# DLRM tower: in the last two batches, four channels of an outer product move to GpSimd, two sums move to VectorE, and the tail steps change places

## The reference, cut to what matters

```python
for i in range(3):                                    # xk = e at first
    z = einsum('bfe,bge->bfge', x, xk)                # outer products over the 16 fields
    z = relu(einsum(z, Ws[i]) + bs[i]).sum(-1)        # 16 numbers per sample
    xk = broadcast(z)                                 # so layers 1 and 2 need only y = x @ Ws[i].T and z
h = concat([z0, z1, z2, dense_ctx], axis=1)           # 48 + 16 = 64 features
h = relu(h @ W_top1 + b_top1)                         # 512
h = relu(h @ W_top2 + b_top2)                         # 256
y = h @ W_top3                                        # 1
```

## Time and profile before

| | |
|---|---|
| median of 3 runs | 578.62 us (578.22 to 579.26) |
| the profiled execution | 579.74 us |
| its span in the profile | 578.0 us |
| VectorE busy | 542.8 us (94%) |
| ScalarE busy | 498.7 us (86%) |
| TensorE matmuls busy | 476.3 us (82%) |
| GpSimd busy | 467.8 us (81%) |
| TensorE's mean granted clock | 0.956 of 2.4 GHz |

### The profile page before, as it was taken

How to read it: one execution, slowest core, us unless ns; L and a number is a source line. 1 busy time by engine, 2 the same in 40 slices (tenths; PEclk the granted TensorE clock), 3 DMA queues, 4 the chain that set the end, 5 groups by cost and what they waited for, 6 DMA issues and landing times.

```text
span 578.0 us, 10773 instructions
## 1 busy us (share of the span) xinstructions
PE 476.3 (82%) x3990; PEld 190.8 (33%) x3990; DVE 542.8 (94%) x326; ACT 498.7 (86%) x1471; POOL 467.8 (81%) x354
## 2 busy tenths in 40 slices
PE   5559888687888798878989788798869888789988
PEld 5213233232333333232333323233333323233324
DVE  1697999999999999999999999999999999999994
ACT  1143698999999999999999999989999999999875
POOL 6665888889888888888888889888888888888630
PEclk9689898999989989998999999799999989999979
DMA  3352212221222122212221222212212212210000
GB/s 98 92 145 74 75 56 57 63 64 56 74 58 64 56 71 72 67 56 74 62 64 56 69 60 61 73 57 82 64 56 66 61 60 74 57 54 1 1 2 0
DMA packets 14334, 35.43 MB, mean 61 GB/s; under 512 B 5493, under 2 KB 5879, under 8 KB 14266
## 3 DMA queue, kind: packets, MB, share of 16 engines
q0 software_dynamic: 12288, 33.57, 20.3%
q1 hardware_dynamic: 1994, 1.17, 0.8%
HBM read 34.71 MB, written 0.01 MB: 60 GB/s over the span
## 4 chain that ended last, share of the span: by engine, by line
DVE 38%; ACT 28%; PE 18%; issue 10%; POOL 3%; another core or an unknown queue 1%; DMA 1%; ACTq 0%; DVEq 0%; POOLq 0%
DVE prod L436 32%; ACT outer L637 15%; PE z_ps L827 8%; DVE outer L485 6%; ACT outer L627 3%; ACT sq L582 3%; POOL x_rows L342 3%; PE t_ps L790 3%; ACT relu L593 2%; ACT xt L574 2%; PE turn_ps L898 1%; PE turn_ps L902 1%; PE turn_ps L860 1%; PE zs_ps L842 1%
## 5 line engine op out<-in xcount | busy, mean ns | idle before, releaser
L436 DVE TENSOR_TENSOR prod<-t_ps,xt 128x2048 f32<-128x2048 f32 x190 | 420.8, 2281 | 11.0 <-remote 6.7
L342 POOL DMA_INDIRECT x_rows<-in_tbl,ids_sb x256 | 248.4, 970 | 73.1 <-issue 62.0
L637 ACT ACTIVATE outer<-outer,bias_sb 128x256 f32<-128x256 f32 x476 | 236.7, 518 | 3.0 <-DVE outer L485 3.0
L827 PE MATMUL z_ps<-prod,w_sb 128*32 128x512 f32 x1520 | 191.2, 622 | 37.3 <-DVE prod L436 34.3
L356 POOL TENSOR_TENSOR intra<-xt 128x1024 f32<-128x1024 f32 (+4 forms) x90 | 205.1, 2281 | 6.0 <-PE z_ps L827 4.5
L574 ACT ACTIVATE xt<-t_ps 128x512 f32<-128x512 f32 x128 | 75.2, 604 | 45.2 <-PE t_ps L790 21.7
L637 ACT ACTIVATION_READ_ACCUMULATOR outer<-outer,bias_sb 128x1 f32 x476 | 100.2, 210 | 0.0
L485 DVE TENSOR_TENSOR outer<-y_ps,z_all 128x1408 f32<-128x1408 f32 (+2 forms) x60 | 93.4, 1598 | 4.5 <-ACT outer L627 3.5
L790 PE MATMUL t_ps<-ident,x_rows 128*128 128x128 f32 x512 | 81.2, 288 | 19.0 <-DMA x_rows<-in_tbl,ids_sb 7.1
L827 PEld LDWEIGHTS z_ps<-prod,w_sb 128*32 128x32 f32 x1520 | 45.8, 111 | 124.8 <-issue 93.3
L790 PEld LDWEIGHTS t_ps<-ident,x_rows 128*128 128x128 f32 x512 | 55.9, 143 | 81.8 <-issue 59.6
(11 more groups left out here) (69 smaller groups left out, 219.1 us busy)
## 6 DMA issues: line engine op xcount, KB each, us to landing
x_rows<-in_tbl,ids_sb POOLq DMA_INDIRECT x256
w_sb<-in_w SPq DMA_DIRECT2D x1, 512.0 KB
feat<-in_dense SPq DMA_DIRECT2D x1, 128.0 KB
w_sb<-in_w SPq DMA_DIRECT2D x1, 128.0 KB
ids_sb<-in_ids SPq DMA_DIRECT2D x1, 120.0 KB
ident<-in_identity SPq DMA_DIRECT2D x1, 64.0 KB, 2.1
w_sb<-in_w0t SPq DMA_DIRECT2D x1, 64.0 KB
sel_sb<-in_sel SPq DMA_DIRECT2D x1, 48.0 KB
```

Of the source, the lines that this page charges most:

```text
L342: pool.indirect_dma_start(out=x_rows[:, par, f, :], out_offset=None, in_=tables[f], in_offset=bass.IndirectOffsetOnAxis(ap=ids_sb[:, NF * ...
L436: dve.tensor_tensor(prod[:, m % PROD_RING, half, :].rearrange("p (f g s) -> p f g s", f=QF, g=QF), t_ps[:, tbank(b, q, half), :, :].unsque ...
L637: act.activation(outer_of(b)[:, o // OP, o % OP, :], outer_of(b)[:, o // OP, o % OP, :], ACT.Relu, bias=bias12_sb[:, layer - 1, o:o + 1], ...
L827: mm = pe.matmul(z_ps[j * GR:(j + 1) * GR, m % 2, 0:n], w0_sb[:, half, slot, :], src[:, half, j * n:(j + 1) * n], start=(slot == 0 and hal ...
```

## The change

- GpSimd gets `outer_former`: channels 12 to 15 of batch 14's layer 2 outer product. It reads a copy of y in SBUF that ScalarE makes with a new `copy_y_former`, between `copy_tile(LAST, 3, 1)` and `move_z0(LAST - 1)`. VectorE's second piece of that outer product shrinks from 8 channels to 4. VectorE's four sums (14, 2) wait for GpSimd.
- VectorE takes 12 of the 16 sums (15, 1) instead of 10, ScalarE 4 instead of 6.
- On ScalarE, the move of `mlp_b` goes ahead of `sum_outer(14, 2, 8, 12)`; the eight sums (15, 2) all go ahead of the move of `mlp_c`, and of `tail_move(0, 4)` and `(0, 5)`, which stood between them.
- On TensorE, `mlp_c` goes from ahead of `tail_h2(0, .)` to behind it; `form_feat(LAST)` goes ahead of `tail_y(0)`; the eight transposes at the end are gone.

```diff
-WARM = {"first": 28, "second": 22, "end": 8}
+WARM = {"first": 28, "second": 22}
-VECTOR_SUMS = {(2, 2): 4, (1, 1): 10, (1, 2): 8}
+VECTOR_SUMS = {(2, 2): 4, (1, 1): 12, (1, 2): 8}
+        y_former = sb("y_former", [P, QF, GROUPS, LAST_OP])
-        def vector_channels(b):
+        def vector_channels(b, layer):
-            return NF - LAST_OP if b == LAST else NF
+            return NF - LAST_OP if (b, layer) > (LAST - 1, 1) else NF
@@ gpsimd
+            def outer_former():
+                pool.wait_ge(y_copied, 1)
+                pool.wait_ge(z_ready, z_count(LAST - 1, 1))
+                o = NF - LAST_OP
+                y = y_former[:, :, :, :].rearrange("p f c o -> p o (f c)")
+                pool.tensor_tensor(
+                    outer[:, o // OP, o % OP:o % OP + LAST_OP, :].rearrange("p o (g f) -> p o g f", g=NF),
+                    y.unsqueeze(2).to_broadcast([P, LAST_OP, NF, NF]),
+                    z_all[:, (LAST - 1) % 2, 1, :].unsqueeze(1).unsqueeze(3).to_broadcast([P, LAST_OP, NF, NF]),
+                    ALU.mult).then_inc(pool_outer, 1)
             multiply_last_unit(1)
+            outer_former()
             outer_last(1)
@@ vector
-                n = op(b)
+                n = min(op(b), vector_channels(b, layer) - o)
                     else:
-                        dve.wait_ge(pool_outer, layer)
+                        dve.wait_ge(pool_outer, 1 if b < LAST else 1 + layer)
-            vector_sum(LAST, 1, 6, 16)
+            vector_sum(LAST, 1, 4, 16)
@@ scalar
+            def copy_y_former():
+                act.wait_ge(y_turned, LAST)
+                act.activation(y_former[:, :, :, :], y_ps[:, :, :, 1, NF - LAST_OP:NF], ACT.Copy).then_inc(y_copied, 1)
             copy_tile(LAST, 3, 1)
+            copy_y_former()
             move_z0(LAST - 1)
...
             sum_outer(LAST - 1, 2, 4, 8)
+            mlp_in(LAST, "mlp_b")
             sum_outer(LAST - 1, 2, 8, 12)
-            mlp_in(LAST, "mlp_b")
             move_feat(LAST - 1)
             sum_outer(LAST, 1, 0, 2)
             sum_outer(LAST, 1, 2, 4)
-            sum_outer(LAST, 1, 4, 6)
             tail_move(0, 0)
             tail_move(0, 1)
             tail_move(0, 2)
             tail_move(0, 3)
+            sum_outer(LAST, 2, 0, 4)
+            sum_outer(LAST, 2, 4, 8)
             mlp_in(LAST, "mlp_c")
-            sum_outer(LAST, 2, 0, 2)
-            sum_outer(LAST, 2, 2, 4)
             tail_move(0, 4)
             tail_move(0, 5)
-            sum_outer(LAST, 2, 4, 6)
-            sum_outer(LAST, 2, 6, 8)
             move_feat(LAST)
@@ tensor
             tail_h1(0, 3)
-            mlp_in(LAST, "mlp_c")
             tail_h2(0, 0)
             tail_h2(0, 1)
             tail_h2(0, 2)
             tail_h2(0, 3)
+            mlp_in(LAST, "mlp_c")
+            form_feat(LAST)
             tail_y(0)
-            pe.wait_ge(turn_moved, turn(LAST + 2, "feat"))
-            keep_warm("end")
-            form_feat(LAST)
             tail_h1(1, 0)
```

More of the change, by code:

```diff
@@ L212, in op @@
             return LAST_OP if b == LAST else OP
-        def vector_channels(b):
-            return NF - LAST_OP if b == LAST else NF
+        def vector_channels(b, layer):
+            return NF - LAST_OP if (b, layer) > (LAST - 1, 1) else NF
         def piece(b, layer, o):
-            return 2 * PIECES * b + vector_channels(b) // op(b) * (layer - 1) + o // op(b)
+            return 2 * PIECES * b + vector_channels(b, 1) // op(b) * (layer - 1) + o // op(b)
         def mlp_slot(frame, kind):
@@ L368, in multiply_last_unit @@
                     ALU.mult).then_inc(pool_multiplied, 1)
+            def outer_former():
[8 more added lines that the diff above has]
+                    ALU.mult).then_inc(pool_outer, 1)
             def outer_last(layer):
                 if layer == 1:
-                    pool.wait_ge(y_copied, 1)
+                    pool.wait_ge(y_copied, 2)
                     pool.wait_ge(z0_moved, NB)
@@ L478, in outer_piece @@
                         dve.wait_ge(y_turned, b + 1)
-                        if b == LAST:
-                            dve.wait_ge(y_copied, 1)
+                        if b >= LAST - 1:
+                            dve.wait_ge(y_copied, b - LAST + 2)
                     if (b, layer) != (LAST, 1):
@@ L491, in outer_pieces @@
             def outer_pieces(b, layer):
-                for o in range(0, vector_channels(b), op(b)):
+                for o in range(0, vector_channels(b, layer), op(b)):
                     outer_piece(b, layer, o)
@@ L498, in vector_sum @@
                 for o in range(first, last):
-                    if o < vector_channels(b):
+                    if o < vector_channels(b, layer):
                         dve.wait_ge(outer_done, piece(b, layer, o) + 1)
                     else:
-                        dve.wait_ge(pool_outer, layer)
+                        dve.wait_ge(pool_outer, 1 if b < LAST else 1 + layer)
                     dve.scalar_tensor_tensor(
@@ L949, in keep_warm @@
             def keep_warm(when):
-                out = turn_ps[:, 0:P] if when == "end" else zs_ps[:, 0:P]
                 for _ in range(WARM[when]):
-                    pe.transpose(out, ident[:, :], ident[:, :])
+                    pe.transpose(zs_ps[:, 0:P], ident[:, :], ident[:, :])
             pe.wait_ge(ident_loaded, 16)
```

## The result

| | before | changed |
|---|---|---|
| median | 579.26 us (574.37 to 582.61, 19 executions) | 582.93 us (580.17 to 586.45 and one of 674.55, 19 executions) |
| ratio of the two | | 1.0078, 95% interval 1.0053 to 1.0104 |
| profiled execution | 579.74 us | 581.73 us |
| its span | 578.0 us | 579.6 us |

One of the 19 executions of the changed kernel took 674.55 us, with a mean clock of 0.735 against 0.91 to 0.96 in the others; it is left out of the ratio, and so are three of the experiments' (586.0 and 586.57 us with the gap filled, 586.75 us for GpSimd and VectorE alone), each over 1.5% above the fastest of its kernel.

The account below looks back on a forecast made before the run. The end was taken as set by `tail_h1(0, 0)`'s start, TensorE's 9.84 us and clock, and the step to `tail_h1(1, 0)`: 557.03 + 9.84 + 4.3, then 2.4, 5.8 and 1.74, gave 581.1, forecast 581.0 us; range 578.9 to 582.8.

Parts of the forecast that it names:

- The part on GpSimd and VectorE: Batch 14 outer product split and sums (15, 1): z of layer 1 ready 2.0 us earlier, hidden behind `mlp_c`.
- ScalarE's wait for `mlp_b`: ScalarE stands 1.4 us for `mlp_b`'s matmuls; `tail_h1(0, 0)` starts at 557.03 instead of 555.58, 1.45 us later.
- The step from `mlp_c`'s end to `tail_h1(1, 0)`: In the tail, `tail_h1(1, 0)` starts 2.4 us after `mlp_c` ends, behind its move and two queued tail moves.
- The whole tail without low clock: With equal clock loss in both kernels, the tail step `tail_h1(1, 0)` starts 0.5 us later than before.
- The low clock over all of `tail_h1`: TensorE's clock at 0.50 from about 557 to about 566, covering `tail_h1` from its start.
- Rivals 3 to 5: TensorE clock stays up, 576.8 us (0.10); last 128 samples at low clock, 583.3 (0.06); GpSimd holds VectorE up, 583.5 (0.04).
- the term L: Time lost to low clock from `tail_h1(0, 0)` to `mlp_c`'s end: 4.3 us taken, bounds 1.7 and 5.1.
- the sum: `mlp_c` ends at 571.2, `tail_h1(1, 0)` starts at 573.6, span ends at 579.4; with 1.74 us outside, 581.1.

Follow-up runs that it names:

- with the gap filled: Changed kernel plus 16 transposes that nobody reads, on TensorE between `mlp_b`'s matmuls and `form_feat(14)`; ratio to the kernel before 1.0026.
- GpSimd and VectorE alone: Kernel before plus `outer_former`, `copy_y_former` and VectorE's 12 sums (15, 1), all ScalarE and TensorE orders as before; ratio 1.0037.
- with `mlp_b` back and the gap filled: Changed kernel with `mlp_b`'s move behind its four sums again and 8 transposes between `mlp_b`'s matmuls and `form_feat(14)`; ratio to before 0.9998.
- e5_before_b_fwd: Kernel before with ScalarE's `mlp_b` move put ahead of the sums (14, 2) of channels 8 to 11; ratio 1.0075.
- the fastest version: Changed kernel, `mlp_b` behind its sums, 8 transposes ahead of `form_feat(14)` and 3 behind, `mlp_c` inside `tail_h1(0)`; 576.64 against 579.67 us, ratio 0.9957.

## Why the prediction was wrong

Right, by its own steps:

- The part on GpSimd and VectorE, and that its 2 us would be hidden: `form_feat(LAST)` came 5.5 us after the last sum.
- ScalarE's wait for `mlp_b`: 1.4 us expected, 1.39 measured. `tail_h1(0, 0)`: expected 12.14 us behind the tail's entry (557.03 - 544.89), measured 12.21.
- The step from `mlp_c`'s end to `tail_h1(1, 0)`: 2.4 expected, 573.82 - 571.3 = 2.5 measured. The whole tail without low clock: 0.5 us longer expected, 0.6 measured.
- The low clock over all of `tail_h1`, from about 557 to about 566: measured 556.1 to 566.4, 10.2 us. The span was expected at 579.4 and measured at 579.6, and that closeness is luck: the execution entered its tail 0.7 us earlier than before's had, and this hid a low stretch that cost 0.8 us more than the sum had.
- Rivals 3 to 5 did not happen: no profile of the changed kernel kept its clock up, the last 128 samples ran at 1.00, and VectorE's pieces of (14, 2) were not held up (3.42 us beside `outer_former`, 3.4 expected).

Wrong was the term L, the time lost to the low clock, in two ways. First its size: "I take 4.3" with 5.1 as the upper bound, and the three profiles of the changed kernel gave 5.1, 5.1 and 3.4, so the value taken as the extreme came twice in three. That is 0.8 us for the profiled execution. (About 0.2 of the 5.1 is not the clock's: the stretch from `tail_h1`'s start to the end of `mlp_c`, 9.84 us at full clock by the sum, took 10.0 us, 566.32 - 556.31, in the profile with `mlp_b` back and the gap filled, which has the same order and no low clock.) Secondly, and more, the step from the profile to the median: "in the changed kernel I expect the long stretch to be the rule, so I shift it hardly". The sum was made against one execution of before that itself had lost 3.4 us to the low clock, while its second profile lost nothing. So it gave the changed kernel 4.3 - 3.4 = 0.9 us of clock, and by leaving out the 1.1 us between that execution and before's median nearly 1 us more: before was taken to lose 2.3 to 2.4 us as a rule. The moved line lengthens the low stretch and also makes it regular: the profiles with `mlp_b` forward and nothing in the gap lost 5.1, 5.1, 3.4 and 4.7 us (in the last, `e5_before_b_fwd`, the low stretch began 1.3 us ahead of `tail_h1`), those of the five kernels and executions with `mlp_b` behind its sums and no transposes in that gap 3.4, 0, 3.4, 0 and 0. The means, 4.6 and 1.4, differ by 3.2, and with the 0.6 of structure and the 0.35 outside the span the change comes to 4.2 us, within the measured interval (3.1 to 6.0 us). The forecast had 1.9 for the first of these three, 0.5 for the second and nothing for the last. The two means rest on four and five profiles and are uncertain by about 1 us; that the sum meets the ratio so closely is in part luck.

The 0.13 us by which the time lies above the range are less than the 0.64 us between before's two medians (578.62 us in 3 executions, 579.26 in 19): counted from the first, the same 3.7 us would have ended at 582.3, inside the range. So that it fell just outside is chance, and the fault in L is not. The range was too narrow for a third reason: it took its scale from three runs of before within 1.0 us, and held nothing for the place at which an execution enters the tail, which was 544.2 to 549.4 us in these profiles. Why it moves is not settled here; the change touches nothing ahead of 529 us, and both kernels show late entries (547.8 before, 549.4 changed).

What stays open beside that: the 0.35 us outside the span, and whether the 1.0037 of the GpSimd part alone is more than those.

## What to carry to other kernels

A move put ahead of other work on an in-order engine gains nothing if what it waits for isn't ready: compare its producer's end (553.68 here) with the time at which the engine would reach it (552.33) before moving it. Where a stage runs on TensorE after a wait, count the wait twice, once as time and once for the clock behind it: here 1.4 us of wait cost about 3 us of clock on the average, an estimate from nine profiles (3.2) and the mean clocks of two series (2.5 and 3.2). A single profile shows one draw of the clock, so ask of each low stretch on the critical path whether the next execution would have it, before making a sum against it.

## What the runs showed of the hardware

- The granted clock fell in the middle of 64-row matmuls: at 558.9 with the gap filled, TensorE having worked for 2.23 us of the 3.60 ahead of 557.3 with hardly a pause since, and at 563.3 in the changed kernel's third profile. The same matmuls ran at 1.00 in five profiles with `mlp_b` behind its sums, so neither they nor the 128-row work mixed in by the fastest version decide it alone.
- One of VectorE's sums, which read two tensors from SBUF, lost 2.2 us where it was issued 0.2 us behind the start of a GpSimd operation (2.69 against 0.48 us), and its pieces with y in PSUM nothing (3.49 against 3.48), as the Trainium skill has it (GPSIMD Engine Reference, Specifications: contention with VectorE instructions of two SBUF inputs).
- A kernel with one GpSimd operation, one ScalarE copy and one SBUF tensor more spent 2.15 instead of 1.8 us outside the profiled span.
